# A MetaFormer layer on 64 images: the second norm's shift formed on GpSimd, and the weights' preparation laid beside the first pairs

## What is computed

```
x = x + conv(_ln_c(x))                       # x: (64, 128, 28, 28); norm over the 128 channels
  # conv, spatial half: theta = _cbr(x, th), phi = _cbr(x, ph); Gs = theta^T phi (784 x 784 per image)
  #   Gs_joint = _cbr(concat(Gs^T, Gs), ggs); g_xs = mean(_cbr(x, gxs)); x *= sigmoid(W(_cbr(ys, ws1)))
  # conv, channel half: the same over 128 x 128 with thc, phc, gxc (weights of 784 inputs), ggc, wc1
t = tokens(x)
router_probs = softmax(_ln_t(t) @ router_w + router_b);  top 2 of 8 experts
t = t + sum of 2 of (_ln_t(t) @ expert_w[e] + expert_b[e]) by normalised weight
```

## Time and profile before

| | us |
|---|---|
| median of 3 runs | 1956.86 |
| lowest and highest | 1954.93, 1962.75 |
| the profiled run, its own time | 1957.01 |
| its span in the profile | 1955.2 |
| TensorE busy | 1840.2 (94%) |
| VectorE busy | 1536.7 (79%) |
| ScalarE busy | 1179.7 (60%) |
| GpSimd busy | 1112.3 (57%) |
| TensorE's granted clock, mean | 0.986 |

### The profile page before, as it was taken

How to read it: one execution, slowest core, us unless ns; L and a number is a source line. 1 busy time by engine, 2 the same in 40 slices (tenths; PEclk the granted TensorE clock), 3 DMA queues, 4 the chain that set the end, 5 groups by cost and what they waited for, 6 DMA issues and landing times.

```text
span 1955.2 us, 39114 instructions
## 1 busy us (share of the span) xinstructions
PE 1840.2 (94%) x13396; PEld 1331.0 (68%) x13396; DVE 1536.7 (79%) x4761; ACT 1179.7 (60%) x3240; POOL 1112.3 (57%) x1169
## 2 busy tenths in 40 slices
PE   3579999999999999999999999999999999999986
PEld 2257777767777776777776677777667777766774
DVE  3447888888888888888888888888888888887666
ACT  2445666666566666656666665666666566666544
POOL 0234656655665655566565556656555665655455
PEclk9799999999999999999999999999999999999998
DMA  4211121121212112121212212121221212121011
GB/s 93 75 43 67 67 84 60 67 76 67 84 67 84 54 73 75 67 84 67 84 51 76 75 68 84 67 84 51 73 78 67 84 67 81 54 68 65 35 51 50
DMA packets 43345, 135.11 MB, mean 69 GB/s; under 512 B 7980, under 2 KB 9597, under 8 KB 43150
## 3 DMA queue, kind: packets, MB, share of 16 engines
q1 hardware_dynamic: 40588, 130.74, 19.1%
q10 hardware_dynamic: 2562, 1.89, 0.4%
HBM read 106.50 MB, written 26.10 MB: 68 GB/s over the span
## 4 chain that ended last, share of the span: by engine, by line
PE 86%; DVE 6%; issue 2%; ACT 2%; DMA 2%; POOL 1%; SPq 0%; DVEq 0%; POOLq 0%; ACTq 0%
PE rot L984 7%; PE rot L994 7%; PE rot L985 7%; PE high L1122 5%; PE low L1122 5%; PE high L1124 4%; PE rot L940 4%; PE low L1124 4%; PE high L1123 4%; PE low L1123 4%; PE rot L920 4%; DVE part L1518 4%; PE rot L1077 3%; PE rot L1113 3%; PE rot L858 3%; PE rot L953 2%
## 5 line engine op out<-in xcount | busy, mean ns | idle before, releaser
L503 POOL TENSOR_TENSOR part<-part 128x256 f32<-128x256 f32 (+1 forms) x416 | 407.7, 980 | 293.1 <-DVE part L1518 290.9
L1518 DVE SCALAR_TENSOR_TENSOR part<-high,gv,part 128x128 f32<-128x128 f32 (+1 forms) x1664 | 459.3, 342 | 120.6 <-ACT part L717 117.5
L717 ACT ACTIVATE part<-low,gv 128x128 f32<-128x128 f32 (+1 forms) x1664 | 467.9, 374 | 136.3 <-POOL otok L508 71.1
L984 PE MATMUL rot<-x1h,wch 112*128 112x256 f32 x1120 | 277.5, 286 | 0.6 <-ACT chan L664 0.6
L985 PE MATMUL rot<-x1h,wcl 112*128 112x256 f32 x1120 | 271.6, 281 | 0.0
L508 POOL TENSOR_TENSOR otok<-part 128x128 f32<-128x128 f32 (+1 forms) x416 | 214.4, 515 | 32.6
L984 PEld LDWEIGHTS rot<-x1h,wch 112*128 112x128 f32 x1120 | 211.5, 189 | 7.1 <-issue 1.6
L985 PEld LDWEIGHTS rot<-x1h,wcl 112*128 112x128 f32 x1120 | 211.8, 189 | 1.3
L478 POOL TENSOR_TENSOR tp_l<-tp,tp_h 128x448 fp32r<-128x448 f32 x64 | 69.4, 1085 | 249.7 <-ACT tp_h L603 249.7
L495 POOL TENSOR_TENSOR x1l<-tok,x1h 112x1024 fp32r<-112x1024 f32 x64 | 136.0, 2124 | 113.5 <-ACT x1h L657 113.5
L1122 PE MATMUL low<-weh,xh 128*128 128x512 f32 (+1 forms) x416 | 180.4, 434 | 4.8 <-ACT part L717 4.8
(11 more groups left out here) (209 smaller groups left out, 3772.7 us busy)
## 6 DMA issues: line engine op xcount, KB each, us to landing
xin<-in_x SPq DMA_DIRECT2D x32, 784.0 KB, 4.3
y_ch<-rstd_rows SPq DMA_DIRECT2D x32, 784.0 KB, 4.0
x<-in_x SPq DMA_DIRECT2D x32, 784.0 KB, 4.3
cen<-shift_rows SPq DMA_DIRECT2D x32, 784.0 KB, 4.0
out<-x SPq DMA_DIRECT2D x64, 392.0 KB, 2.3
otok<-in_ggs_w SPq DMA_DIRECT2D x1, 600.2 KB
y_ch<-in_ggs_w SPq DMA_DIRECT2D x1, 600.2 KB
j<-in_expert_w SPq DMA_DIRECT2D x1, 512.0 KB
```

The lines of the kernel that those rows point to most:

```text
L503: nc.gpsimd.tensor_tensor(part[0:n, slot, 0:2, :], part[0:n, slot, 0:2, :], part[0:n, slot, 2:4, :], ALU.add).then_inc(sem("half_sum"), 1)
L717: last = nc.scalar.activation(part[0:n, turn % RING, e, :], low[turn % 2][0:n, e * C:(e + 1) * C], ACT.Copy, scale=gv[par(p, back)][0:n, i ...
L984: nc.tensor.matmul(dst, wch[:, j, rows], hi_x, start=(j == 0), stop=False)
L1518: last = nc.vector.scalar_tensor_tensor(out=own, in0=high[turn % 2][0:n, e * C:(e + 1) * C], scalar=gv[par(p, back)][0:n, i, HALF + e:HALF ...
```

## The change

There are three edits. First, `shifts` is gone from VectorE; its two operations stand in GpSimd's `inverse_std2`, behind the power. Second, the preparation is cut into functions that steps call: `wide_weights(0)` to `(4)` and `late_weights` in step n = 2, `expert_weights` in step n = 3, each at the same place of all engines' sequences, with VectorE's `wide_scales` at the end of step n = 1. They use the `low` and `high` banks (`spaces`), which are not otherwise used so early. `space_weights` (ggs, w3, ws1) still comes before the first step. Third, `step(0, 1, ahead=True)` is called on every engine before that: it holds only the back-1 work of pair 0 up to the rstd row, and the steps leave that out for the pair (`opening`). SP issues 12 of the wide loads behind the small ones, then rstd's write and read, then 14 more wide loads and the experts'. VectorE's memsets come first.

```
         def opening(k, p, back):
+            return isinstance(k, int) and 2 * k + p == back
...
-            for dst, src in expert:
-                sp.dma_start(dst, src).then_inc(sem("expert_loaded"), 16)
+            for dst, src in wide[0:12]:
+                sp.dma_start(dst, src).then_inc(sem("wide_loaded"), 16)
...
+            step(sp, 0, 1, ahead=True)
+            for dst, src in wide[12:]:
+                sp.dma_start(dst, src).then_inc(sem("wide_loaded"), 16)
+            for dst, src in expert:
+                sp.dma_start(dst, src).then_inc(sem("expert_loaded"), 16)
             steps(sp, step)
...
                         nc.gpsimd.tensor_tensor(rstd2[:, :], var2[:, :], mhalf[:, 0:TILES], ALU.pow)\
                             .then_inc(sem("rstd2_ready"), 1)
+                        need(pool, "rstd2_ready", k, p, 1, back)
+                        nc.gpsimd.tensor_tensor(std2[:, :], var2[:, :], rstd2[:, :], ALU.mult).then_inc(sem("std2_ready"), 1)
+                        need(pool, "std2_ready", k, p, 1, back)
+                        nc.gpsimd.tensor_tensor(shift[:, :], mean2[:, :], std2[:, :], ALU.subtract)\
+                            .then_inc(sem("shift_ready"), 1)
...
-            for dst, src in wide:
+            for dst, src in big:
                 act.dma_start(dst, src).then_inc(sem("wide_loaded"), 16)
...
+            def wide_weights(m):
+                pe.wait_ge(sem("wide_scaled"), m + 1)
+                for q, (j0, j1_) in enumerate(QUART):
+                    n = 2 * m + q
+                    if n < 4:
+                        pe.wait_ge(sem("space_read"), 11 + n)
+                    else:
+                        pe.wait_ge(sem("wch_ready"), n - 3)
+                        pe.wait_ge(sem("wcl_ready"), n - 3)
+                    t = spaces[(15 + n) % 4]
...
+                if ahead:
+                    x_tokens(0, 0, 1)
...
+                    rstd_turn(1)
+                    return
...
                 tp_tokens(0, 2)
+                if 2 * k + p == 2:
+                    wide_weights(0)
                 low_half(7, 5)
                 gx(1, 2)
+                if 2 * k + p == 2:
+                    wide_weights(1)
...
                 high_half(12, 5)
+                if 2 * k + p == 3:
+                    expert_weights()
                 channels0_high(3)
...
+            step(pe, 0, 1, ahead=True)
+            space_weights()
+            pe.wait_ge(sem("small_read"), 1)
             steps(pe, step)
...
+            def wide_scales():
+                dve.wait_ge(sem("wide_loaded"), 16 * len(big + wide))
...
                 x1_tokens(1, 3)
-                shifts(4)
+                if 2 * k + p == 3:
+                    expert_weights()
                 gate_high(9, 5)
                 gate_high(10, 5)
+                if 2 * k + p == 2:
+                    wide_weights(0)
+                    wide_weights(1)
                 stats1(0, 1)
                 stats1(1, 1)
                 moments1(1)
+                if 2 * k + p == 2:
+                    wide_weights(2)
+                    wide_weights(3)
```

More of the change, by code:

```diff
@@ L407, in rstd_out @@
                 def rstd_out(back):
-                    row_out("rstd", rstd_row, back)
+                    if ahead or not opening(k, p, back):
+                        row_out("rstd", rstd_row, back)
                 def rstd_in(back):
-                    if live(k, p, back):
+                    if live(k, p, back) and (ahead or not opening(k, p, back)):
                         need(sp, "tp_filled", k, p, 2, back + 1)
@@ L458, in _, with step @@
                                     base=0, pattern=[[-1, 128]], channel_multiplier=1).then_inc(sem("ident_ready"), 1)
-            def step(pool, k, p):
+            def step(pool, k, p, ahead=False):
                 def inverse_std1(back):
-                    if live(k, p, back):
+                    if live(k, p, back) and (ahead or not opening(k, p, back)):
                         need(pool, "stats1_ready", k, p, 1, back)
@@ L533, in step @@
                 add_token(6, 4)
+            step(pool, 0, 1, ahead=True)
             steps(pool, step)
@@ L777, in step @@
                 space_copy(2)
+            step(act, 0, 1, ahead=True)
+            space_weights()
             steps(act, step)
@@ L827, in _ @@
-            last.then_inc(sem("small_filled"), 1)
-            pe.wait_ge(sem("cleared"), 4)
-            pe.wait_ge(sem("expert_loaded"), 16 * len(expert))
-            for i in range(2):
-                half = slice(i * HALF, (i + 1) * HALF)
-                nc.tensor.matmul(low[i][:, :], avg[:, :], raw_we[:, half, :].rearrange("p e c -> p (e c)"),
-                                 start=True, stop=False)
-                nc.tensor.matmul(low[i][:, :], neg_avg[:, :], raw_eb[:, i * 512:(i + 1) * 512], start=False, stop=True)\
-                    .then_inc(sem("centre_filled"), 1)
@@ L845, in width, with step @@
+            def step(pe, k, p, ahead=False):
                 def width(q):
@@ L913, in mixed @@
                     if live(k, p, back):
+                        if opening(k, p, back):
+                            pe.wait_ge(sem("space_read"), 2 * NT)
                         free(pe, "mix", k, p)
@@ L1037, in joint_c @@
                     if live(k, p, back):
+                        if opening(k, p, back):
+                            pe.wait_ge(sem("late_read"), 1)
                         free(pe, "jc", k, p)
@@ L1089, in logits @@
                     if live(k, p, back):
+                        if opening(k, p, back):
+                            pe.wait_ge(sem("weights_ready"), 1)
                         free(pe, "logit", k, p)
@@ L1296, in step @@
+            def step(dve, k, p, ahead=False):
                 count = [0]
@@ L1580, in step @@
                 residual(1, 0, 3)
+                if 2 * k + p == 1:
+                    wide_scales()
+            step(dve, 0, 1, ahead=True)
+            space_weights()
             steps(dve, step)
```

351 lines of the change are left out of this document (204 added, 147 removed).

## The result

| | before | after |
|---|---|---|
| median of the runs, us | 1958.55 (1954.93 to 1962.75, 4 runs) | 1915.41 (1912.15 to 1917.23, 4 runs) |
| span of the profiled execution, us | 1955.2 | 1910.1 |
| one step in the middle (mean of 24 distances between shift transposes), us | 57.16 | 56.75 |
| TensorE busy from 1000 to 1500 us | 493.38 | 496.31 |

The changed kernel takes 0.9782 of the time of before, interval [0.9767, 0.9797]: 43 us less. The forecast was 1913 us, range 1902 to 1930. The total is right to 2 us, and still neither of its two large terms has the size that was put down for it. The 45.1 us between the two profiled spans lie in five places, found by laying the starts of the 32 shift transposes of both traces side by side: 27.8 us up to the first one, 1.6 up to the second, 11.3 up to the thirtieth (28 steps of 0.40), 4.1 in the last two steps, 0.3 behind.

The account below looks back on a forecast made before the run. The middle was taken as bound by TensorE's own work plus its wait for VectorE's shift, with an idle opening outside it. 1957.0 - 22 (shift) - 21.7 (opening) = 1913 us, range for 8 in 10 1902 to 1930.

Parts of the forecast that it names:

- What would show it: List of signs: shift wait gone, step 56.5 us, short GpSimd rows, first theta at 34 to 37 us, second at 64 to 68.
- one sign of being wrong: Middle: TensorE waits for something else; listed beside late small weights and a first full step over 35 us.
- Part 1: Shift pair moved to GpSimd: TensorE's whole 0.665 us wait per step goes, 22 us in all, bounds 11 to 25.
- What is late next?: Middle, after the shift: nearest candidate is low_half(2), waiting for ScalarE's gating; 0.02 us per step taken off.
- the next wait takes over: Rival, middle: TensorE reaches low_half(2) before its gate; 0.35 us per step comes back, 11 us, giving 1924; chance 0.15.
- The first shift wait: First shift transpose: its wait is bigger, 5.30 us, and the new pair gives back some 2.0.
- The drain: End of the run, outside the middle: the change hardly touches it; no separate term.
- Part 2: Opening: first theta 31.6 us earlier, less 4.6 and 5.3 given back, 21.7 us gained; bounds 13 and 28.
- The 1.6 us put down for the clock at theta: Opening: TensorE's transposes right ahead of theta avoid the 0.50 clock at which it was 2.62 us long; 1.6 back.
- The first full step: Opening: wide weights and the second pair's later x load give back 3.7 + 2.5 - 1.6 = 4.6 us.
- The slower one: Rival, GpSimd: the pair is as dear as the power, 4.9 us; each step 1.3 us longer, 1975 us; chance 0.05.
- The queue rival: Rival, opening: SP issues wide scales only after the rstd row, which small loads delay; 1923 us; chance 0.13.

Follow-up runs that it names:

- vector_early: Kernel before, with the shift pair kept on VectorE but put ahead of its second half of x1; 1946.23 us, ratio 0.9947.
- dear1: Changed kernel with one more 2.44 us power, into a tile nothing reads, ahead of the pair on GpSimd; 1921.80 us, ratio 0.9823.
- shift_only: Kernel before, with only the shift pair moved from VectorE to GpSimd behind the power, opening as before; 1940.55 us, ratio 0.9918.
- loads_first: Changed kernel with all wide and expert loads on SyncE's queue ahead of the first pair's row; 1923.14 us, ratio 0.9821.
- no_ahead: Changed kernel with the first pair's tokens, statistics and row made in its own step, behind the space weights; 1932.91 us, ratio 0.9886.
- serial: Changed kernel with wide, late and expert weights prepared in one piece behind the space weights, before the first pair's own step; 1930.66 us, ratio 0.9862.

## Why the prediction was right, and where it wasn't

**What would show it.** Held: the shift wait is gone; two GpSimd rows of 13 columns under 0.5 us (0.21 and 0.22; 0.3 each was put down). Not held: the step of 56.5 us (56.75), theta of the first pair at 34 to 37 us (32.08), of the second at 64 to 68 (61.87), the third's some 22 us ahead (25.8). And one sign of being wrong came true: TensorE waits in the middle for something else.

**Part 1, 22 us: the step that failed is "What is late next?".** That the little subtraction on VectorE stood still while GpSimd worked was right, and vector_early shows it without changing the engine. That the pair is hidden on GpSimd was right with room: 2.5 us more cost nothing (dear1). The relief was even larger than its term (0.85 us in the ledger, 0.665 put down). But for what is late next the text took 0.02 us per step, and 0.45 us went back, in two places. One is the low and high products that wait for the routing's gates: 0.28 us and not 0.02, of which 0.10 at the low product that it named and the rest at a high product that it didn't. I had read it from TensorE's list of waits (1.4 us in 2 cases), and a chain that is just in time doesn't stand in such a list. The other it missed: the copy of the theta and phi tokens ended 0.65 us before the mixing matmuls in the kernel before, and 0.14 is what is left between them where TensorE waits for it, so it had 0.5 us to spare; and its chain (x-token copies, x1 cast, x1l, token, gates) came forward by less than TensorE did. The middle brought 0.40 us x 28 = 11 us, where the text's 0.645 makes 18. The rival "the next wait takes over" had about the size (0.35 us per step given back; 0.25 is missing from the step, 0.45 by the ledger) and a part of the place. The first shift wait brought the 2 us put down for it: shift_only starts that transpose 2.5 us earlier.

**The drain, "which the change hardly touches", brought 4 us** in the profiled pair of runs; the sum has its last two steps in it like all others, for 1.3. In the next to last step the shift wait was 1.39 us and not 0.66, and a gate of VectorE that stood behind the pair made the next product wait 0.68 us; both are gone. Another 1.3 us lie between the last step's first transposes and its shift transpose, where TensorE's granted clock was 0.72 in the trace of before (1894 to 1900 us) and 1.00 in that of after (1850 to 1856 us). shift_only shows 2.4 us from the thirtieth to the last shift transpose.

**Part 2, 21.7 us: right within what the runs can tell** (24, interval 21 to 27). Inside it terms are off that partly cancel. The small weights landed at 23.0 us and not at 26.6 as before, and VectorE took 3.5 us up to the transposes and not 4.2; so theta of the first pair came 35.3 us earlier, not 31.6. Why the weights landed earlier was not tried. In loads_first, no_ahead and serial VectorE starts on them at 23.1 to 23.5 too, so it is not the call ahead nor the row's place in the queue; what all of these share is that ScalarE issues 7 loads beside SyncE's small ones and no longer 33, and that VectorE's memsets come first. The 1.6 us put down for the clock at theta were misread: its four matmuls took 1.76 us and not 2.62, but at the same low clock, 0.95 to 1.01 us each in both kernels. In the kernel before VectorE still normalised the second image while theta ran; now it was done before. The first full step gave back 3.6 us (4.6 put down), the next 5.9 (5.3 for the expert matmuls).

**Rivals.** The slower one was real but 2.5 us away, and priced up to 20 us too cheap. For GpSimd's arithmetic the Trainium skill (GPSIMD Engine Reference, Engine selection) gives about twice VectorE's time for two inputs; at 13 columns the rows show 213 ns against VectorE's 169, a quarter more. The queue rival's mechanism was there in small: SyncE stood 3.88 us at one load, and the wide scaling waited 1.37 us.

The total was right partly by luck: by the ratios of the parts the shift with its share of the drain came 6 us short of its term, the opening 2 us over, and the whole 3 us over the sum of the two (by the medians 5 short, 3 over and 1).

## What to carry to other kernels

Where an engine is relieved of a wait, list for each of its next inputs when it is ready and when it is asked for, and not only the inputs that it already waits for: the ones with under a wait's length to spare take the gain. A small VectorE instruction whose duration is ten times its twin's, and that ends with a GpSimd subtraction, is a wait in disguise; move it or the subtraction, and look for the next such place at once. A fix at the waiting instruction can lose until the shared resource behind it is freed, so try the two together before dropping either.

## What the runs showed that I had not expected

Moving one copy forward, which removed the only regular wait of TensorE, made the kernel 13 us slower; with two GpSimd instructions moved it made the same kernel 13 us faster (1908.55 to 1895.27). GpSimd's subtraction held VectorE's small two-input operations (0.17 to 2.34 us, 0.26 to 3.14), while its power, as long as the subtraction, did not (0.27 beside it). The text ahead of the prediction says that the engines meet only at semaphores; here two of them met without one. And a clock of 1.00 at the start of a profile can be a missing record: the 14 transposes at 5.57 us took 3.21 us, as at 0.50, though the view gives 1.00. The time of a known instruction tells it.
